# One decoder layer on one core: two heads' scores of the third key tile in one bank, halved transposes of a row's second output pair, and a new table of urgencies

## The reference

```python
x = layernorm(x + self_attention(x))           # rope, in_proj, causal softmax, out_w
x = layernorm(x + cross_attention(x, ctx))     # 154 keys, bias, rotated q and k
x = layernorm(x + moe(x))                      # top 2 of 8 experts, silu(x w1) * (x w3) -> w2

scores = einsum('bqhd,bkhd->bhqk', qh, kh) / sqrt(8)
scores = where(causal, scores, -inf)
attn = softmax(scores); o = einsum('bhqk,bkhd->bqhd', attn, vh) @ out_w.T + out_b
```

## Time and profile before

| | us |
|---|---|
| median of 3 runs | 249.91 |
| lowest, highest | 249.85, 252.05 |
| the profiled execution's own time | 248.22 |
| its span, first to last instruction | 246.4 |
| TensorE busy in it | 232.7 |

### The profile page before, as it was taken

The page is one execution under the profiler, slowest core; times in us unless marked ns, Lnnn a source line. Parts: engine busy times, 40 slices in busy tenths (PEclk is TensorE's granted clock), DMA queues, the critical chain, the costliest instruction groups (busy, mean ns, idle before and its releaser), DMA issues.

```text
span 246.4 us, 4685 instructions
## 1 busy us (share of the span) xinstructions
PE 232.7 (94%) x1438; PEld 164.7 (67%) x1438; DVE 186.0 (75%) x631; ACT 161.3 (65%) x332; POOL 89.1 (36%) x161
## 2 busy tenths in 40 slices
PE   7999999999999999999999999988899999999981
PEld 3456668666666776677765576553588878987860
DVE  5558987989879899986876898990399763348974
ACT  2488785889778779897898734747368765022234
POOL 9998547241432453355221211174011000470300
PEclk9999999999999999999999999999999999999998
DMA  6990002000003100000221000011311101010101
GB/s 237 340 330 3 1 1 85 3 1 4 0 0 117 56 1 3 1 0 3 81 87 60 32 1 3 0 53 58 106 32 44 45 21 54 25 53 11 39 7 43
DMA packets 10568, 12.57 MB, mean 51 GB/s; under 512 B 1200, under 2 KB 7728, under 8 KB 10416
## 3 DMA queue, kind: packets, MB, share of 16 engines
q1 hardware_dynamic: 9456, 10.43, 12.9%
q0 software_dynamic: 512, 1.05, 1.4%
q10 hardware_dynamic: 576, 0.79, 0.9%
HBM read 9.25 MB, written 3.01 MB: 50 GB/s over the span
## 4 chain that ended last, share of the span: by engine, by line
PE 80%; DVE 10%; ACT 4%; issue 3%; DMA 2%; DVEq 0%; ACTq 0%; SPq 0%
PE psB L1083 12%; PE psA L1054 12%; PE psO L1106 10%; PE psJ L952 3%; PE psJ L1186 3%; PE psJ L990 3%; PE psJ L953 3%; PE psJ L1067 2%; PE psA L1249 2%; PE psO L1111 2%; PE psO L982 2%; PE psJ L1065 2%; PE psA L1231 2%; PE psJ L997 1%; DMA xT<-xt_dram 1%
## 5 line engine op out<-in xcount | busy, mean ns | idle before, releaser
L1576 DVE CUSTOM_DVE_ANT_0 junk<-psA,c 128x128 bf16<-128x128 f32 (+3 forms) x128 | 55.7, 487 | 8.8 <-PE psA L1054 8.4
L1348 ACT ACTIVATE prob<-psB 128x512 f32<-128x512 f32 (+1 forms) x88 | 47.4, 558 | 13.6 <-PE psB L1083 11.8
L1083 PE MATMUL psB<-qb,kst 128*128 128x512 f32 (+3 forms) x128 | 38.0, 338 | 0.2 <-ACT prob_more L1348 0.2
L1054 PE MATMUL psA<-kst,qa 128*128 128x512 f32 (+1 forms) x88 | 36.6, 425 | 0.0
L1083 PEld LDWEIGHTS psB<-qb,kst 128*128 128x128 f32 x128 | 22.8, 189 | 11.4 <-issue 4.3
L1581 DVE TENSOR_REDUCE negm<-psA 128x3 f32<-128x462 f32 (+1 forms) x48 | 26.4, 579 | 4.5 <-PE psA L1054 3.9
L1348 ACT ACTIVATE prob_more<-psB 128x512 f32<-128x512 f32 (+1 forms) x48 | 24.5, 527 | 6.1 <-PE psB L1083 5.9
L1392 ACT ACTIVATE silu<-psA 128x512 f32<-128x512 f32 x16 | 9.6, 599 | 24.4 <-DVE hid L1739 18.0
L899 POOL TENSOR_SCALAR_AFFINE_SELECT prob<-prob 128x256 f32<-128x256 f32 x32 | 13.0, 408 | 31.3 <-ACT prob_more L1348 31.3
L1054 PEld LDWEIGHTS psA<-kst,qa 128*128 128x128 f32 x88 | 16.4, 188 | 6.0 <-issue 3.9
L1106 PE MATMUL psO<-prob_more,v 128*32 128x512 f32 (+3 forms) x128 | 20.3, 439 | 0.0
(11 more groups left out here) (198 smaller groups left out, 562.6 us busy)
## 6 DMA issues: line engine op xcount, KB each, us to landing
c<-w_dram SPq DMA_DIRECT2D x8, 256.0 KB, 2.6
w<-w_dram SPq DMA_DIRECT2D x1, 1024.0 KB, 4.7
xs_dram<-kst SPq DMA_DIRECT2D x1, 960.0 KB, 7.2
ys_dram<-ys SPq DMA_DIRECT2D x7, 128.0 KB, 1.8
rest<-xs_dram SPq DMA_DIRECT2D x3, 256.0 KB, 2.8
c<-c_dram SPq DMA_DIRECT2D x1, 666.0 KB, 8.5
xT<-xt_dram SPq DMA_DIRECT2D x2, 256.0 KB, 4.7
x_tok<-x_dram SPq DMA_DIRECT2D x1, 512.0 KB, 9.5
```

What stands on the lines that cost most here:

```text
L1054: last = nc.tensor.matmul(ps[:, c:c + heads * width].rearrange("p (n w) -> p n w", n=heads), qa[:, u % SLOTS, 128 * i:128 * i + 128], keys ...
L1083: last = nc.tensor.matmul(ps[:, c:c + S - 128 * kt], keys, qb[:, u % 2, 128 * kt:S], start=m == 0, stop=m == len(blocks) - 1, skip_group_c ...
L1348: nc.scalar.activation(dst, psB[n % SIZE["B"]][:, 0:cols], ACT.Exp, scale=SCALE).then_inc(b_done[n % SIZE["B"]], 1)
L1576: last = nc.vector.tensor_tensor_reduce(out=junk[:, p, cols], in0=psA[p][:, cols], in1=c32[:, C_MASK + S - width:C_MASK + S], scale=-1.0, ...
```

## The change

Three things. In stage 0 the third key tile's scores of two heads (256 columns each) now stand in one bank and one exponential takes both, through a three-dimensional view, since in `prob` the two heads lie 1280 columns apart: 10 fills and 10 exponentials a unit for 12. Of a row's second pair (p odd) the item OT is split into two, each with two transposes and its own bank of psJ, and VectorE divides by halves; ONT of a half waits for its own half. And the table `EARLY` is a new one, with which every engine's order is a new one. VectorE's CQ also waits for the low part of the piece before, which it wrote itself.

```diff
--- before.py
+++ after.py
@@ -98,15 +98,15 @@
 def b_fills(u):
 
     if unit(u)[0] == 0:
-        kinds = (((0, 0),), ((1, 0), (3, S - 128)), ((2, 0),))
-        return [tuple((kt, j, c) for kt, c in tiles) for tiles in kinds for j in range(G)]
+        kinds = (((0, 0),), ((1, 0), (3, S - 128)))
+        return [tuple((kt, j, c) for kt, c in tiles) for tiles in kinds for j in range(G)] + [((2, j, 0), (2, j + 1, 256)) for j in range(0, G, 2)]
     return [((0, j, 0),) for j in range(G)] + [((1, None, 0),)]
 
 
 def exps_of(u, kt):
 
     if unit(u)[0] == 0:
-        return {0: range(4), 1: range(4, 8), 3: range(4, 8), 2: range(8, 12)}[kt]
+        return {0: range(4), 1: range(4, 8), 3: range(4, 8), 2: range(8, 10)}[kt]
     return {0: range(4), 1: [4]}[kt]
 
 
@@ -125,6 +125,11 @@
 
 def last_pv(u):
     return ("PV", (u, len(BURSTS[unit(u)[0]]) - 1))
+
+
+def turns(p):
+
+    return [("OT", (p, h)) for h in range(2)] if p % 2 else [("OT", (p,))]
 
 
 def masks(u, kt):
@@ -264,14 +269,16 @@
         if g % 2 == 0:
             continue
         p = u // 2
-        add("POC", (p,), [("ACT", 0.49)], [last_pv(u)] + ([(("OT", (p - 1,)), 0)] if p else []))
-        add("OT", (p,), [("PE", 0.44), ("DVE", 0.8)], [("POC", (p,)), ("LOAD", (3,))],
-            [(1, ("ONT", row(u - NG) + (1,)))] if g == 1 and u >= NG else [])
+        add("POC", (p,), [("ACT", 0.49)], [last_pv(u)] + ([(turns(p - 1)[-1], 0)] if p else []))
+        for item in turns(p):
+            whole = len(item[1]) == 1
+            add("OT", item[1], [("PE", 0.44), ("DVE", 0.8)] if whole else [("PE", 0.24), ("DVE", 0.5)], [("POC", (p,)), ("LOAD", (3,))],
+                [(1, ("ONT", row(u - NG) + (1,)))] if g == 1 and u >= NG else [])
         if g < NG - 1:
             continue
 
         for h in range(2):
-            add("ONT", (st, b, h), [("PE", 0.24), ("ACT", 0.3)], [("OT", (p,))],
+            add("ONT", (st, b, h), [("PE", 0.24), ("ACT", 0.3)], [("OT", (p, h)), ("OT", (p - 1,))],
                 [(1, (("OP", row(u - NG) + (h,)), 0))] if u >= NG else [])
             add("OP", (st, b, h), [("PE", 0.48), ("DVE", 0.38)], [("ONT", (st, b, h)), ("XB", ()) if st == 0 else ("XO", (b,))],
                 [(1, ("LNX", row(u - NG) + (h,)))] if u >= NG else [])
@@ -421,17 +428,19 @@
 EARLY = {
...
-    ('F2', 3): -30, ('F2', 4): -20, ('H', 1, 'k'): -596, ('H', 1, 'q'): 125, ('LNX', 0, 0, 0): 6, ('MP', 12): 12,
...
+    ('R3', 10): 173, ('R3', 11): 63, ('R3', 12): -22, ('R3', 4): -6, ('R3', 5): 16, ('RT',): -1, ('SC', 2): -364,
...
 }
@@ -1113,17 +1122,18 @@
                     if k == len(BURSTS[st]) - 1:
                         last.then_inc(s_pv, 1)
                 elif kind == "OT":
-                    p, = args
+                    p = args[0]
                     loaded(s_id, 16)
                     ps = bank(JOB[item])
                     pe.wait_ge(s_po, p + 1)
-                    for i in range(QT):
+                    for i in range(QT) if len(args) == 1 else (2 * args[1], 2 * args[1] + 1):
                         last = nc.tensor.transpose(ps[:, 128 * i:128 * i + 128], po_sb[:, 128 * i:128 * i + 128], ident)
                     last.then_inc(j_full, 1)
                 elif kind == "ONT":
                     st, b, h = args
                     ps = bank(JOB[item])
-                    job_done(pe, "OT", NG // 2 * (2 * st + b + 1) - 1)
+                    job_done(pe, "OT", NG // 2 * (2 * st + b + 1) - 2)
+                    job_done(pe, "OT", NG // 2 * (2 * st + b + 1) - 1, h)
                     for i in (2 * h, 2 * h + 1):
                         last = nc.tensor.transpose(ps[:, 128 * i:128 * i + 128], onorm[:, i, :], ident)
                     last.then_inc(j_full, 1)
@@ -1339,18 +1349,23 @@
                         act.wait_ge(s_pv, u - 1)
                     act.wait_ge(s_b, n + 1)
                     kt, j, _ = b_fills(u)[k][0]
-                    if st == 0:
-                        half, first = (prob, prob_more)[j // 2], j % 2 * 1280 + [0, 512, 1024][kt]
-                        cols = 256 if kt == 2 else 512
-                        dst = half[:, u % 2, first:first + cols]
+                    scores = psB[n % SIZE["B"]][:, :]
+                    if st == 0 and kt == 2:
+
+                        dst = (prob, prob_more)[j // 2][:, u % 2, :].rearrange("p (j c) -> p j c", j=2)[:, :, 1024:1280]
+                        scores = scores.rearrange("p (j c) -> p j c", j=2)
+                    elif st == 0:
+                        half, first = (prob, prob_more)[j // 2], j % 2 * 1280 + [0, 512][kt]
+                        dst = half[:, u % 2, first:first + S]
                     else:
-                        cols, dst = S, prob_at(u, kt, j)
-                    nc.scalar.activation(dst, psB[n % SIZE["B"]][:, 0:cols], ACT.Exp, scale=SCALE).then_inc(b_done[n % SIZE["B"]], 1)
+                        dst = prob_at(u, kt, j)
+                    nc.scalar.activation(dst, scores, ACT.Exp, scale=SCALE).then_inc(b_done[n % SIZE["B"]], 1)
                 elif kind == "POC":
                     p, = args
                     act.wait_ge(s_pv, 2 * p + 2)
                     if p:
-                        job_filled(act, ("OT", (p - 1,)))
+                        for other in turns(p - 1):
+                            job_filled(act, other)
                     nc.scalar.activation(po_sb[:, :], psO[:, :], ACT.Copy).then_inc(s_po, 1)
                 elif kind == "ONT":
                     st, b, h = args
@@ -1583,17 +1598,22 @@
                                                        negate=True)
                     last.then_inc(a_done[p], 1)
                 elif kind == "OT":
-                    p, = args
+                    p = args[0]
                     ps = bank(JOB[item])
                     if p % 2 == 0 and p:
-                        job_filled(dve, ("ONT", divmod(p // 2 - 1, 2) + (1,)))
-                    o = ps[:, :].rearrange("p (i j h c) -> p i j h c", i=QT, j=G, h=2)
-                    link(nc.vector.reciprocal(rec[:, p % 2, :], ps[:, :].rearrange("p (n c) -> p n c", c=V_AT)[:, :, HD]))
-                    sums = rec[:, p % 2, :].rearrange("p (i j h) -> p i j h", i=QT, j=G)
+                        for h in range(2):
+                            job_filled(dve, ("ONT", divmod(p // 2 - 1, 2) + (h,)))
+
+                    tiles = slice(0, QT) if len(args) == 1 else slice(2 * args[1], 2 * args[1] + 2)
+                    n = tiles.stop - tiles.start
+                    o = ps[:, :].rearrange("p (i j h c) -> p i j h c", i=QT, j=G, h=2)[:, tiles]
+                    at = slice(2 * G * tiles.start, 2 * G * tiles.stop)
+                    link(nc.vector.reciprocal(rec[:, p % 2, at], ps[:, :].rearrange("p (n c) -> p n c", c=V_AT)[:, at, HD]))
+                    sums = rec[:, p % 2, at].rearrange("p (i j h) -> p i j h", i=n, j=G)
                     for h in range(2):
                         first = 32 * (p * 2 % NG + h)
-                        ins = nc.vector.tensor_tensor(onorm[:, :, first:first + 32].rearrange("p i (j d) -> p i j d", j=G), o[:, :, :, h, 0:HD],
-                                                      sums[:, :, :, h].unsqueeze(3).to_broadcast([128, QT, G, HD]), ALU.mult)
+                        ins = nc.vector.tensor_tensor(onorm[:, tiles, first:first + 32].rearrange("p i (j d) -> p i j d", j=G), o[:, :, :, h, 0:HD],
+                                                      sums[:, :, :, h].unsqueeze(3).to_broadcast([128, n, G, HD]), ALU.mult)
                     free(JOB[item], ins)
                 elif kind == "OP":
                     st, b, h = args
@@ -1626,6 +1646,8 @@
                     cols = slice(256 * h, 256 * h + 256)
                     ps = bank(n)
                     dve.wait_ge(s_hi, pieces(PART["x", b])[0])
+
+                    dve.wait_ge(s_lo, pieces(PART["x", b])[0] - PART["c",])
                     for k, c in enumerate((C_CQ, C_SQ)):
 
                         ins = nc.vector.scalar_tensor_tensor(out=ps[:, 256:512] if k else rest[:, 0, cols], in0=ps[:, 256 * k:256 * k + 256],
```

## The result

| | before | after |
|---|---|---|
| median, us | 250.41 (16 runs, 249.56 to 252.13) | 253.03 (16 runs, 251.55 to 255.53) |
| the profiled execution's own time, span | 248.22, 246.4 | 253.46, 251.7 |

The ratio is 1.0093, 95% interval 1.0064 to 1.0122: slower by about 1%, where 248.5 us (245.6 to 251.6) was forecast. The three runs shown of before belong to these 16.

The account below looks back on a forecast made before the run. The prediction took TensorE, busy 94% of the span, to bound the kernel. Its terms, -0.5 + 0.4 - 0.5 + 0 - 0.4 - 0.4 + 0 = -1.4 us, took 249.9 to 248.5 us, range 245.6 to 251.6.

Parts of the forecast that it names:

- The base: Starting time 249.9 us: median of the runs shown, 1.7 above the profiled execution's 248.22; the terms were added to it.
- Pairing, -0.5: Stage 0, third key tile: one exponential for two heads shortens TensorE's waits for ScalarE, -0.5 us (0 to -1.6).
- rival B: Whole kernel: edits do what they say but do not reach the end, TensorE full; 0 to -0.3 us, 249.7; chance 0.17.
- Halves, +0.4: OT of second pairs split: more VectorE time, on the path only at unit 11's pair, +0.4 us (0 to +0.93).
- Order between the stages, -0.5: Before SQ of unit 12: 1.2 us more cover, 0.6 lost to a WS, so the wait for CQ2 closes: -0.5 us.
- Stage 0's order, -0.4: From 60 to 136 us: the new order wins small TensorE gaps, -0.4 us (-1.5 to +1.5).
- From there to the end of stage 1 the path is fixed, 15.2 us: From `place_u` through scatters, landings and loads to the first XS: 15.2 us that no edit touches, so 0.
- The tail, -0.4: At the end: two F2 now apart on VectorE, removing TensorE waits of 0.35 and 0.40 us, -0.4 us.
- Rival D: At 145 to 150 us: two fillers fewer let the clock fall, costing 4 us, time 252.5; chance 0.03.
- Rival C: Near 136 us: the WS moved ahead of CQ and CQ2 waits for its DMA, +2.9 us, 252.8; chance 0.15.
- the signs of being wrong that the prediction named: Strided exponentials over 0.6 us, ScalarE idle near 136, `place_u` after 160, TensorE idle over 0.5 (12 to 136), clock under 1.00.

Follow-up runs that it names:

- before, first: The kernel before, unedited, in the profile the prediction was made from: own time 248.22 us, span 246.4.
- after, third: The changed kernel again, unedited, on a chip without late signals: 247.44 us beside 247.87 for the kernel before, ratio 0.9976.
- before, second: The kernel before again, unedited, on a chip with late signals: median 250.81 us, profiled span 250.0.
- after, second: The changed kernel again, unedited, on a chip with late signals: 252.57 us beside 250.60 for the kernel before, ratio 1.0077.
- the crossed tables: `EARLY` exchanged: changed kernel with old table 255.90 us, kernel before with new table 267.47, changed kernel with old urgencies for the experts only 251.54; kernel before 250.60.
- the order joined at XS: Both edits, every engine in the changed kernel's order up to the first XS, then the kernel before's: 247.04 us, ratio 0.9972 to the kernel before; repeated, 0.9975.
- three pieces: Both edits; changed kernel's order to the first XS, kernel before's to F3,6, changed kernel's from there: 250.23 us beside 250.77 for the kernel before, ratio 0.9964.

## Why the prediction was wrong

The step that failed is the sum's account of the experts' phase. It held the path from `place_u` to the first XS for fixed and had one term behind it, -0.4 for the order at the end. With late signals the routed tiles take 1.4 us more in after's order and the tail 1.6 to 2.4 more. The part up to `place_u` came out near its forecast, but by luck: two of its terms were wrong by more than they were worth, and the order made up for them.

| stretch, us | forecast | before, first, to after, third (not late) | before, second, to after, second (late) |
|---|---|---|---|
| to the first score matmul | none | -0.58 | -0.17 |
| to `place_u` | -1.0 | -0.77 | -0.55 |
| to R1 of tile 0 | 0 | -0.27 | -0.01 |
| to F3,6 | none | +1.38 | +1.38 |
| the tail | -0.4 | -0.96 | +1.56 |
| behind it | none | +0.10 | +0.09 |
| span | -1.4 | -1.1 | +2.3 |

The first row is not the change's doing. Without it the left column is -0.5, and the medians differ by -0.4.

**The base.** The prediction added 1.7 us, the median over the profiled execution. That gap was no constant: before takes 247.4 to 248.7 where signals are not late and 249.3 to 252.2 where they are. By its time and its waits the profile came from the first kind, by their times the three runs from the second. Beside the 16 runs this base was only 0.5 too low (250.41 for 249.91); what it hid is a wait that the profile does not show.

**Pairing, -0.5: wrong.** Counted from the first score it gains nothing (+0.1). ScalarE does save its time (62.97 us busy from 60 to 136 us instead of 64.20), but the waits that this was to shorten, 5.4 us of B's weight loads for ScalarE, stayed. With the pairing, 20 to 118 us:

```profile
PEld psB L1255 <- ACT prob L1524: 4.0, 8, 0.8
PEld psB L1255 <- ACT prob_more L1524: 1.6, 6, 0.4
```

This is rival B for this term. It holds for a fill at the first head's place and an exponential at the second's; other places were not tried. The strided output costs nothing: the 40 exponentials into `prob_more`, 8 of them over 2 x 256, have a mean of 598 ns; the 32 contiguous ones in before's second profile have 599.

```profile
L1362 ACT ACTIVATE prob_more<-psB 128x512 f32<-128x512 f32 x40 | 23.3, 598 | 7.9 <-PE psB L1092 7.5
...
L1615 DVE TENSOR_TENSOR c<-psJ,rec 128x64 f32<-128x64 f32 x16 | 2.8, 220 | 0.3
...
L1611 DVE RECIPROCAL rec<-psJ 128x16 f32<-128x16 f32 x8 | 2.0, 252 | 0.8 <-PE psJ L1130 0.8
```

**Halves, +0.4: the sizes right, the mechanism missed.** 252 ns against 270 estimated, 220 against 220. But the old order pays 1.75 us up to `place_u`, far above the bound of 0.93, and in every stretch with a split pair (0.5, 0.5, 0.8), not only at unit 12. The bound counted VectorE's instructions alone; what the trace shows is TensorE waiting for turns of a two-bank ring, which I named in one clause and gave no price. At unit 12 these waits are 0.22 and 0.29 of the 0.8; the rest is not settled. In after's order a score block stands between the halves, and from SQ of unit 12 to `place_u` it takes 20.1 us, against 19.9 before and 20.8 with the halves in the old order. That the block between them does it was not tested by itself.

**Order between the stages, -0.5: the size near, not as argued.** From unit 8's B to SQ of unit 12 after takes 0.4 us less than before. But the gap was to close, and TensorE still waits 0.52 us for CQ2:

```profile
138.11 0.47 PE L961 MATMUL psJ<-high,fr 128*128 128x512 f32 x1 [0.52 <-DVE low L1561]
```

The cost of the WS moved in front of it was taken as 0.64 us. It took 1.72, beside GpSimd's addition XO, which began at 134.80 and lasted 1.38; in before XO ran at 137.01 beside CQ2, whose 0.72 against its twin's 0.41 I had put down to nothing.

```profile
134.64 0.41 DVE L1561 TENSOR_TENSOR low<-rest,high 128x256 fp32r<-128x256 f32 x1
135.02 1.72 DVE L1534 TENSOR_TENSOR wp<-c,wp 128x512 fp32r<-128x512 f32 x1
...
137.77 0.69 DVE L1534 TENSOR_TENSOR wp<-c,wp 128x512 fp32r<-128x512 f32 x1
```

```profile
134.80 1.38 POOL L860 TENSOR_TENSOR x_tok<-x_tok,brow 128x512 f32<-128x512 f32 x1 [6.29 <-DVE rest L1657]
```

The Trainium skill, "SBUF — State Buffer", section "SBUF: two separate sides", says that VectorE, for an operation with two SBUF inputs, and GpSimd share one pair of ports and that the loser waits. Both placements agree; 1.03 us is what it cost VectorE here.

**Stage 0's order, -0.4: too small.** Up to unit 8's B after's order takes 0.9 to 1.2 us less than the old one with both edits. Over the three stretches the order gives 2.3 to 2.5 us where -0.9 was forecast, and that hid the halves.

**"From there to the end of stage 1 the path is fixed, 15.2 us": right only without late signals.** From the end of `place_u` to the first XS the profiles without them take 14.9 us (before's first 15.2), those with them 16.1 to 16.4, and 17.5 to 17.8 where the clock fell as well, as in the second profiles of both (the crossed tables left aside). In after's first profile:

```profile
158.24 0.17 DVE L1716 CAST place_u<-place_f 128x8 uint32<-128x8 f32 x1
```

```profile
174.55 0.60 PE L1231 MATMUL psJ<-c,rest 128*128 128x128 f32 x4
```

**The experts' phase: no term.** I priced two F2 at the end and nothing else. R1 of tile 0 to F3,6 takes 1.4 us more in every profile of the table with after's order there and none with before's. Of it 0.7 is the wait of R3,9 at 197.21, 1.30 us by starts where the longest of before is 0.61, and 0.3 a wait at R1,4; the rest is spread and not settled.

**The tail, -0.4: right without late signals, wrong with.** Without them after's tail is 1.0 us shorter (23.13 to 22.17) and both waits of the earlier trace rows are gone. With them before's tail grows by 1.1 and after's by 3.7 to 4.5. Behind F3,8 before has F1,11, F3,9, F2,2, F1,12 and F2,3 on TensorE ahead of F3,10; after has F2,2, F3,9 and F1,11. That is two items fewer, F1,12 and F2,3. F3,10 needs the bank that VectorE's `hid` of F3,8 frees, and that waits for F2,2's signal. Two things differ. F2,2 ends later in before: in its second profile the last matmul starts at 224.51 and the signal comes at 225.76, 1.25 us behind it, the last gather having landed at 225.63; in after it had been waiting since 222.25. And before has the two items more to do meanwhile. So before reaches F3,10 without a wait there, after does not, and then the clock fell too.

Rival D had the clock, at the wrong place: not the fillers, a wait behind a DMA. The granted clock fell to its lower level behind idle times of 2.67, 2.09, 2.00 and 1.84 us in the tail, and between 172.8 and 179.0 us in three profiles, behind waits of 1.14 to 1.34 us; in others as long a wait there (1.35 at 170.92 in after's first) left it in full. The Trainium skill, "TensorE: Matmul & The Clock Gate", section "HAM oscillation", says that idle gaps make it fall. It is a large part of what late signals cost. Of 69 executions of before on the three chips with late signals, 40 with a mean clock of 0.992 or more take 250.0 us (median) and 29 with 0.991 or less 251.9; on the two other chips none of 58 is that low. Of after's 28 executions with late signals 20 are at 0.991 or less.

Rival C did not occur: ScalarE does not wait for a WD near 136 us. Of the signs of being wrong that the prediction named, two came: TensorE idle by 0.9 us between 12 and 136 us, and the clock. Without late signals the change gains 0.4 us in the medians, with them it loses 2.0 to 2.6.

No order measured is shown best on both kinds of chip: without late signals the order joined at XS has 0.9972 and 0.9975, and after 0.9976; with them three pieces has 0.9964. Three pieces without, and the join at XS with late signals, were not run.

## What to carry to other kernels

Where a median stands 1% above the profile's own time, find out what the other executions wait for before you price a change by the profile. Compare starts between two profiles from a common event behind the first loads, not from the span's start: here 0.6 us of a supposed gain stood before it. Behind a run of indirect DMAs, keep a few microseconds of TensorE's work ahead of anything that needs a signal of another engine; an order that is faster on an undisturbed chip can lose more than it gains where this cover is thin. Halving an item costs a turn of the ring it stands in, whatever its instructions cost; an order with other work between the halves paid less here, though what made it so was not isolated.
